# GpSimd multiplies two neighbouring tiles of a scan's ring in one instruction

## What is computed

```python
xz = x @ in_proj_w.T                      # xp and z, 512 columns each
xc = silu(causal_conv(xp))
dt, Bm, Cm = split(xc @ x_proj_w.T)       # 64, 16 and 16 columns
delta = softplus(dt @ dt_proj_w.T + dt_proj_b)
dA = exp(delta[..., None] * A)            # A = -exp(A_log), (512, 16)
BX = delta[..., None] * Bm[:, :, None, :] * xc[..., None]
h[t] = dA[t] * h[t - 1] + BX[t]           # along the 1024 rows of a batch row
y = sum_n(h[..., n] * Cm[..., n]) + D * xc
out = (y * silu(z)) @ out_proj_w.T
```

## Time and profile before

| | |
|---|---|
| median of 3 runs | 3532.34 us (3526.29 to 3543.96) |
| span of the profiled execution | 3531.4 us |
| busy, share of the span: PE | 2995.4 us, 85% |
| POOL | 2784.6 us, 79% |
| DVE | 2547.8 us, 72% |
| ACT | 2415.2 us, 68% |
| mean granted clock of TensorE | 0.924 |

### The profile page before, as it was taken

One profiled execution on the slowest core, in us unless ns is written; L12 is line 12 of the kernel. 1 busy time (PEld: TensorE's weight loads), 2 busy tenths in 40 slices (PEclk: granted clock), 3 DMA queues, 4 the chain that ended last, 5 costly groups with the idle time before them and its releaser, 6 DMA issues.

```text
span 3531.4 us, 58034 instructions
## 1 busy us (share of the span) xinstructions
PE 2995.4 (85%) x17392; PEld 1873.5 (53%) x17392; DVE 2547.8 (72%) x5923; ACT 2415.2 (68%) x5331; POOL 2784.6 (79%) x2583
## 2 busy tenths in 40 slices
PE   5888888888989988898898889889898998987557
PEld 3555454554655656465565646556464654654236
DVE  3356879787777768777686777867777776879870
ACT  5577778676877767677686767767676776865431
POOL 1118989888888889888898888988898888977880
PEclk9999999999999999999999999989999999998778
DMA  3017878778887888877787788878878778899981
GB/s 75 7 53 204 231 204 230 208 216 254 213 234 199 223 233 216 250 205 216 219 228 233 207 250 213 234 209 218 239 213 251 208 204 230 219 263 260 293 241 38
DMA packets 423336, 736.59 MB, mean 209 GB/s; under 512 B 53426, under 2 KB 100146, under 8 KB 423026
## 3 DMA queue, kind: packets, MB, share of 16 engines
q1 hardware_dynamic: 423026, 732.89, 73.9%
HBM read 648.84 MB, written 83.89 MB: 207 GB/s over the span
## 4 chain that ended last, share of the span: by engine, by line
PE 53%; POOL 14%; issue 9%; DVE 8%; ACT 8%; DMA 6%; SPq 2%; ACTq 0%; DVEq 0%; POOLq 0%
PE bank L483 17%; PE bank L491 7%; POOL u_rows L1523 7%; PE bank L606 6%; POOL u_rows L1516 5%; PE bank L753 5%; PE bank L687 4%; DMA w<-in_mlp_w2T 4%; PE bank L739 3%; PE bank L516 3%; PE bank L528 3%; DVE u_rows L1304 2%; ACT prob L808 2%; PE bank L544 2%; DMA u_rows<-u_dram 2%
## 5 line engine op out<-in xcount | busy, mean ns | idle before, releaser
L1523 POOL TENSOR_TENSOR u_rows<-u_rows,c_rows 128x512 f32<-128x512 f32 x1024 | 1300.9, 1274 | 173.1 <-DVE state L1309 114.7
L1516 POOL TENSOR_TENSOR u_rows<-u_rows,b_rows 128x512 f32<-128x512 f32 x960 | 1221.7, 1274 | 148.1 <-DMA u_rows<-u_dram 132.3
L979 ACT ACTIVATE bank<-d_rows,a_rep 128x512 f32<-128x512 f32 x1024 | 695.5, 688 | 271.7 <-DMA d_rows<-delta_dram 153.0
L1304 DVE TENSOR_TENSOR_SCAN u_rows<-bank,state,u_rows 128x512 f32<-128x512 f32 x512 | 642.9, 1272 | 80.9 <-ACT bank L979 64.1
L1304 DVE TENSOR_TENSOR_SCAN u_rows<-bank,u_rows 128x512 f32<-128x512 f32 x512 | 622.5, 1216 | 90.4 <-ACT bank L979 66.6
L808 ACT ACTIVATE prob<-prob,neg_max 128x256 f32<-128x256 f32 x1024 | 509.6, 504 | 17.4 <-DVE neg_max L1091 17.4
L528 PE MATMUL bank<-ident,prob 128*128 128x128 f32 x2048 | 326.6, 289 | 99.6 <-ACT prob L808 72.1
L1091 DVE CUSTOM_DVE_ANT_0 prob<-bank,band 128x256 f32<-128x256 f32 x896 | 336.1, 417 | 103.2 <-PE bank L516 68.8
L528 PEld LDWEIGHTS bank<-ident,prob 128*128 128x128 f32 x2048 | 239.9, 146 | 269.4 <-issue 214.3
L687 PE MATMUL bank<-u_rows,sum_n 128*32 128x512 f32 x2048 | 289.9, 640 | 85.5 <-POOL u_rows L1523 77.9
L516 PE MATMUL bank<-kT,q_own 32*128 32x256 f32 x2048 | 294.3, 406 | 22.1 <-DVE yg L1318 7.9
(11 more groups left out here) (170 smaller groups left out, 4920.7 us busy)
## 6 DMA issues: line engine op xcount, KB each, us to landing
u_rows<-u_dram SPq DMA_DIRECT2D x1024, 256.0 KB, 5.6
d_rows<-delta_dram SPq DMA_DIRECT2D x1024, 256.0 KB, 5.6
w<-in_W SPq DMA_DIRECT2D x28, 1024.0 KB, 8.1
zs_dram<-region_b SPq DMA_DIRECT2D x64, 256.0 KB, 4.5
xc_dram<-region_b SPq DMA_DIRECT2D x64, 256.0 KB, 3.6
u_dram<-region_b SPq DMA_DIRECT2D x64, 256.0 KB, 5.3
delta_dram<-region_b SPq DMA_DIRECT2D x64, 256.0 KB, 5.4
yg<-xc_dram SPq DMA_DIRECT2D x64, 256.0 KB, 4.1
```

The source lines that it names most:

```text
L979: e.activation(banks[at.bank][:, :], delta_of(i, k), ACT.Exp, scale=a_rep[:, j:j + 1]).then_inc(filled[at.bank], 1)
L1304: e.tensor_tensor_scan(rows, banks[at.bank][:, :], rows, state[:, k:k + 1] if i % 2 else 0.0, ALU.mult, ALU.add).then_inc(drained[at.bank], 1)
L1516: e.tensor_tensor(rows, rows, b_rows[:, :], ALU.mult).then_inc(bx_ready.sem, 1)
L1523: e.tensor_tensor(rows, rows, c_rows[:, :], ALU.mult).then_inc(hc_ready.sem, 1)
```

## The change

POOL takes two neighbouring tiles of the ring, k and k + 1 with k even, in one instruction of 128 x 1024 elements, with the B rows or the C rows read twice by a step of zero. For B, the pair stands where tile k stood (step 10 + 2k - 4) and waits for the loads of both tiles; in the last two groups POOL still takes its even tiles one by one. For C, the offset `OUT_AT` goes from 2 to 4, so that the pair stands where tile k + 1 stood (step 10 + 2k + 4), and it waits for the scans and, in even groups, the kept states of both tiles. All waits count on semaphores that each tile raises as before, POOL's by two at once. The ring, its loads and every other engine's program are the same.

```diff
-SCAN0, LOAD_AT, INPUT_AT, DECAY_AT, KEEP_AT, OUT_AT, SUM_AT, GATE_AT = 10, -10, -4, -2, 1, 2, 8, 10
+SCAN0, LOAD_AT, INPUT_AT, DECAY_AT, KEEP_AT, OUT_AT, SUM_AT, GATE_AT = 10, -10, -4, -2, 1, 4, 8, 10
...
         def pool_scan(e, i):
+            def pair_of(k):
+                at = (i * TILES + k) % U_RING
+                return u_rows[:, at:at + 2, :]
+
+            def twice(rows):
+                return rows.rearrange("p (o t) -> p o t", o=1).broadcast_to([P, 2, G])
+
             def times_b(k):
                 rows = rows_of(i, k)
                 e.wait_ge(*landed(u_landed, i * TILES + k))
-                e.tensor_tensor(rows, rows, b_rows[:, :], ALU.mult).then_inc(bx_ready.sem, 1)
+                if shared_inputs(i, BATCH):
+                    e.tensor_tensor(rows, rows, b_rows[:, :], ALU.mult).then_inc(bx_ready.sem, 1)
+                else:
+                    e.wait_ge(*landed(u_landed, i * TILES + k + 1))
+                    e.tensor_tensor(pair_of(k), pair_of(k), twice(b_rows[:, :]), ALU.mult).then_inc(bx_ready.sem, 2)
 
             def times_c(k):
-                rows = rows_of(i, k)
                 e.wait_ge(*gone(uses["scan", i, f"d{k}"]))
+                e.wait_ge(*gone(uses["scan", i, f"d{k + 1}"]))
                 if i % 2 == 0:
-                    e.wait_ge(*states_kept(i, k + 1))
-                e.tensor_tensor(rows, rows, c_rows[:, :], ALU.mult).then_inc(hc_ready.sem, 1)
+                    e.wait_ge(*states_kept(i, k + 2))
+                e.tensor_tensor(pair_of(k), pair_of(k), twice(c_rows[:, :]), ALU.mult).then_inc(hc_ready.sem, 2)
...
-                if k is not None and not (k % 2 and shared_inputs(i, BATCH)):
+                if k is not None and k % 2 == 0:
...
                 k = tile_at(step, OUT_AT)
-                if k is not None:
+                if k is not None and k % 2 == 0:
```

## The result

The changed kernel takes 3657.47 us (median) beside 3529.4 of the kernel before on the same chip: a ratio of 1.0352, 95% interval 1.0328 to 1.0376. The profiled execution has a span of 3654.5 us, 123.1 more than before. Slower was right; the size is 2.5 us above the top of the range. Medians and ratios are those of fast executions: one of the twelve of the last experiment took 4579 us at a mean granted clock of 0.645 and is left out.

What follows compares the result with a forecast made beforehand. PE was taken to bound the kernel, with GpSimd counting only where PE waits for it. Terms 36 + 24 + 13 + 8 - 3 = 78 us, on 3531.4 plus 0.9, gave 3610 us; range 3540 to 3655.

Steps and rivals of the forecast that it cites:

- The price of a pair: On GpSimd, a pair costs 2.31 us against 1.233 per single multiplication, saving 0.16 us per pair.
- Stretch 1: GpSimd from tile 27's landing to `rden_wide` (L1430): 3.0 us later in 12 groups, +36 us.
- The prediction's own sign of being wrong: At PE's wait for `rden_wide`: the forecast is wrong if L550 waits 3 us or less.
- Stretch 2: GpSimd from L1457 to the sums of tiles 52 to 55: 1.7 us later in 14 groups, +24 us.
- Behind it: Behind tile 63's late load, PE's sums of tiles 56 to 59 come 1.1 us later in 12 groups, +13 us.
- the clock: PE's clock after the wait at L550: a longer wait may cost a slow step, +8 us in 12 groups (0 to 20).
- Scans 0 and 1: GpSimd nearly always busy, but an extra tile ahead of L1430 and `aT`: taken as 0, between -6 and +4 us.
- The last two scans and the tail: In the last scan, without attention, GpSimd is the chain; pairing C saves 5 us at most, taken as -3 us.
- the ring (d): Rival: later sums release loads later, GpSimd's idle time before B doubles and reaches PE: 132 us, 3664 us; chance 8%.
- The others: Rivals: (a) cheaper instructions win, 3500 us, 10%; (b) they cancel, 3546 us, 10%; (c) only the tail, 3561 us, 14%.

Runs made afterwards that it cites:

- the last experiment: The kernel before, with PE turning the identity matrix 62 times ahead of the layer norm and 26 ahead of the MLP weights: 3511.8 us, ratio 0.9938.
- the two fillings tried here: The kernel before, with PE turning the identity matrix in waits ahead of the MLP: 44 and 28 times, 3528.7 us; 62 and 26 times, 3511.8 us.

## Why the prediction was right in direction and short in size

- **The price of a pair**: right. 2360 ns long, starts 2.31 us apart (1614.06 and 1616.37). That it pays for a quarter of what the order costs is shown by the run with one tile per instruction.
- **Stretch 1** (tile 27 to `rden_wide`): right, +3.1 us per group for 3.0. The wait at L550 was forecast near 6 us and is 2.27, since PE now loses time at the sums ahead of it; the lateness at its end is the same. The prediction's own sign of being wrong, a wait of 3 us or less at L550, came up in eight of the 14 groups: it left out the wait at the sums of tiles 20 to 23 that stands in the same list.
- **Stretch 2** (from L1457): right, +1.7 from the fifth `rden_wide` to the MLP, and C54,55 to 0.04 us. L1457's own wait did not grow (49.8 us for 63.7): GpSimd waits for loads just ahead of it. That cost nothing. Nor did the weights move by all of it: their wait lost 11.8 us.
- **Behind it, and the clock**: this is the step that failed, in size. I charged the wait at the sums of tiles 56 to 59 with 1.1 us and the clock with 8 us in all, and left tile 27's landing where it was. In its place the runs show 12 x 3.2 = 39 us where I had 13 + 8 = 21. From the first MLP product to the second L676 behind it PE takes 13.6 us for 11.1 (means of 12 groups): 1.58 us are the wait at the sums (1.3 to 1.8), 19 us in all, and 0.9 us are slower matmuls, some 11 in all. Some 10 us more are DVE's instructions for `mean`, for which I had nothing. The wait stands right behind PE's long waits for the layer norm and the weights. Scan 7, one of the dearest, after:

```profile
1944.93 3.75 PE L483 MATMUL bank<-nb,w 128*128 128x512 f32 x4 [2.48 <-DMA w<-in_mlp_w2T]
1950.09 1.94 PE L687 MATMUL bank<-u_rows,sum_n 128*32 128x512 f32 x8 [1.40 <-POOL u_rows L1534]
...
1953.82 6.72 PE L483 MATMUL bank<-nb,w 128*128 128x512 f32 x12
1960.38 1.02 PE L676 MATMUL bank<-dbc,pick_b 96*128 96x512 f32 x2
```

and before:

```profile
1888.13 3.75 PE L483 MATMUL bank<-nb,w 128*128 128x512 f32 x4 [3.33 <-DMA w<-in_mlp_w2T]
1891.82 1.33 PE L687 MATMUL bank<-u_rows,sum_n 128*32 128x512 f32 x8
...
1894.04 5.31 PE L483 MATMUL bank<-nb,w 128*128 128x512 f32 x12
1899.19 1.02 PE L676 MATMUL bank<-dbc,pick_b 96*128 96x512 f32 x2
```

Here it is 15.45 us after and 11.06 before; of the 4.4 us only 1.40 are the wait, and the rest is slower matmuls: the twelve in the middle take 6.72 us for 5.31. The windows (busy time of PE first, the clock third from the right), after and before:

```profile
1950.00:1954.00 4.00, 3.91 (x11) 1.22 (x12) 0.86 (x3) 2.08 (x4) 3.92 (x5) 0.50 1.05 271
1954.00:1958.00 4.00, 4.00 (x8) 1.73 (x7) 1.44 (x9) 1.28 (x2) 4.00 (x2) 0.67 0.67 216
```

```profile
1888.00:1892.00 4.00, 3.87 (x8) 1.36 (x12) 2.13 (x2) 0.69 (x1) 3.24 (x3) 0.50 1.07 400
1892.00:1896.00 4.00, 4.00 (x15) 1.45 (x11) 1.25 (x4) 3.17 (x7) 3.92 (x5) 0.95 1.06 287
```

The clock stays at 0.50, 1.2 GHz of the two levels, until it rises between 1954 and 1958, 9 to 13 us behind the start of the first product; before, the slice that begins 4 us behind that start has 0.95. The Trainium skill's TensorE: Matmul & The Clock Gate (HAM oscillation) tells of a kernel that falls back to the half rate at the wait of every round. These rows agree: behind the wait for the weights both kernels run at 0.50.

Not all groups are like scan 7. In six of the 12 the clock rises late or falls once more, and the twelve products take 5.5 to 6.8 us; in the other six, scan 6 among them, they take 5.3 as before, though the wait at the sums is as long (1.68 us in scan 6):

```profile
1742.23 5.32 PE L483 MATMUL bank<-nb,w 128*128 128x512 f32 x12
```

What tells the two kinds apart stays open, so that a short wait behind a long one holds the clock down is a guess from half of the groups. The MLP that ends an odd scan stands ahead of an even group's landing: PE loses 3.1 us at it, and with the 1.7 us of `mean` that goes through route and fetch into the landing (+5.0). The one that ends an even scan loses 1.9 us, and the landing behind it is 1.5 us later. PE's 53.5 us of longer matmuls are thus not to be added to the pieces of the table: part of them lies inside, part ends in waits that got shorter.

- **Scans 0 and 1**: taken as 0 beyond stretch 2, measured 13.7 us, against some 3. A wait for `aT` that was 3.07 us is 5.7. **The last two scans and the tail**: forecast -3, measured +12; 10.1 of it at the sums, for which PE waits 74.7 us in place of 64.6. There B is not paired, and in the run with C pairs alone these scans lost 5 us: the DMA engines are full, so a later sum goes straight into the next load. That reading was not tried by itself.
- **Rivals**: the ring (d) spoke of doubled idle time ahead of B, which tripled, and its 3664 us is nearest. The run with C pairs, whose sums are as late in order, has no such idle time, and the second wait alone doubles it; tile 27's loads are late because the fetch is. But the pair of tiles 26 and 27 has only 85.9 of the 429.3 us. The pairs at tiles 8, 12, 16, 44, 54 and 60 have 215 us, where before there were 6, and the loads from tile 12 on do wait for sums. What the ring adds beyond the pieces of the table is not shown, and they leave it little room. The others fell.

## What to carry to other kernels

Fewer, larger instructions on an in-order engine are judged by what is queued around them: list what stands ahead of each instruction that another engine waits for, on every in-order engine that takes part, before and after. A landing time is no fixed point; follow it back to what issues the load, since a microsecond lost by PE can come back through a fetch. An instruction that is longer can also hold up another engine's: compare the durations of its neighbours' instructions, not only their waits. And a wait costs its length and the matmuls behind it at half clock: of the two fillings tried here, the one nearly held to the waits gained 0.6%, and the one that outlasted them 0.2% with an interval that all but reaches nothing.

## What the runs showed that was not expected

- Turning a 128 x 128 identity matrix 62 times in PE's idle time took 6.99 us at the full clock, and with 26 more in the next wait the four products behind took 1.88 us in place of 3.75; started at the half clock, 28 took 5.32 us.
- Two DVE instructions of 128 x 2 elements, 0.16 and 0.17 us long by themselves, took up to 2.28 us beside GpSimd's pairs: each ended just behind a GpSimd instruction.
- In one and the same order, of the 137 us by which pairs shorten GpSimd's busy time (2786.7 to 2649.7), some 40 reached the end.
